# The two transfers that carry a batch's split row maxima are issued from GpSimd in place of SyncE

## The reference

```
mod = silu(c) @ wmod  ->  sa, ca, ga, sb, cb, gb      (per batch; |ga|, |gb| at least 0.25)
h = layernorm(x) * (1 + ca) + sa
q, k, v = h @ W_qkv.T, in 16 heads of 8 features
s = q k.T / sqrt(8) - slope[head] * (j - i), causal mask
x = x + ga * (softmax(s) v) @ W_o.T
h = layernorm(x) * (1 + cb) + sb
x = x + gb * moe(h)
moe: layer norm, router softmax over 8 experts, expert 0 with W1, W2, the other
     seven with one common perturbed pair W1', W2' (the largest and smallest 5% / 2
     of the entries by size changed by 0.8 of themselves); gelu between them
```

## Time and profile before

| what | value |
|---|---|
| median of 3 runs | 331.47 us (329.23 to 332.78) |
| profiled execution, its own time | 329.19 us |
| its span in the trace | 327.4 us |
| mean granted TensorE clock | 0.868 |
| busy: PE / DVE / ACT / POOL | 229.8 / 213.2 / 151.3 / 127.2 us |
| DMA, mean over the span | 62 GB/s |

### The profile page before, as it was taken

The page is one execution under the profiler, slowest core; times in us unless marked ns, Lnnn a source line. Parts: engine busy times, 40 slices in busy tenths (PEclk is TensorE's granted clock), DMA queues, the critical chain, the costliest instruction groups (busy, mean ns, idle before and its releaser), DMA issues.

```text
span 327.4 us, 5318 instructions
## 1 busy us (share of the span) xinstructions
PE 229.8 (70%) x1785; PEld 154.5 (47%) x1799; DVE 213.2 (65%) x681; ACT 151.3 (46%) x337; POOL 127.2 (39%) x204
## 2 busy tenths in 40 slices
PE   2741775288178456739739748878598399999995
PEld 1330554166056334617526625544335166767675
DVE  1662999469447818927955784699958548656264
ACT  1211433258256627716745664584454264343430
POOL 8320499227126314302511421234362582606050
PEclk9999995569879959966985985899879589999999
DMA  7737572502502500430250250000000000101011
GB/s 209 165 82 204 146 243 81 147 0 67 146 0 58 149 7 1 132 82 2 74 136 2 64 149 1 2 3 2 2 2 1 2 0 1 34 1 35 0 32 32
DMA packets 17551, 20.43 MB, mean 62 GB/s; under 512 B 1445, under 2 KB 15412, under 8 KB 16316
## 3 DMA queue, kind: packets, MB, share of 16 engines
q1 hardware_dynamic: 15476, 19.11, 21.8%
q10 hardware_dynamic: 2048, 0.98, 1.1%
HBM read 14.70 MB, written 5.26 MB: 61 GB/s over the span
## 4 chain that ended last, share of the span: by engine, by line
PE 40%; DMA 24%; DVE 15%; POOL 9%; SPq 6%; issue 4%; ACT 2%; POOLq 0%; DVEq 0%
DMA Qs<-nmT 13%; PE bank L746 9%; PE bank L728 9%; DMA parts<-part 6%; PE bank L653 4%; DVE msk L939 4%; SPq L275 3%; DVE nmax L970 3%; POOL hid L390 3%; PE bank L632 2%; DMA Ks<-parts 2%; DMA w_sb<-in_w 2%; PE bank L808 2%; PE bank L627 2%; PE bank L610 2%
## 5 line engine op out<-in xcount | busy, mean ns | idle before, releaser
L403 POOL TENSOR_SCALAR_AFFINE_SELECT PT<-PT 128x256 f32<-128x256 f32 (+1 forms) x96 | 47.3, 496 | 118.2 <-ACT PT L453 116.0
L970 DVE TENSOR_REDUCE nmax<-bank 128x2 f32<-128x512 f32 x64 | 43.8, 684 | 48.4 <-PE bank L610 48.3
L453 ACT ACTIVATE PT<-bank 128x512 f32<-128x512 f32 x96 | 53.9, 587 | 39.1 <-PE bank L627 36.8
L627 PE MATMUL bank<-Qs,Ks 80*128 80x128 bf16 x128 | 14.5, 244 | 38.1 <-DMA Qs<-nmT 38.1
L374 POOL TENSOR_TENSOR ex<-eul,lg 128x32 f32<-128x32 f32 x4 | 21.7, 5427 | 27.9 <-DVE lg L1030 27.9
L610 PE MATMUL bank<-Ks,Qs 78*128 78x256 bf16 x128 | 30.0, 323 | 0.0
L627 PEld LDWEIGHTS bank<-Qs,Ks 80*128 80x128 bf16 x128 | 10.0, 109 | 40.8 <-DMA Qs<-nmT 39.2
L632 PE MATMUL bank<-Qs,Ks 80*128 80x256 bf16 x128 | 28.5, 309 | 0.7 <-ACT PT L453 0.5
L606 PE MATMUL bank<-mask 128*128 128x256 bf16 x64 | 20.5, 320 | 10.4 <-DVE nmax L970 9.8
L653 PE MATMUL bank<-PT,Vx 128*32 128x256 f32 x256 | 24.0, 452 | 5.4 <-POOL PT L403 5.2
L966 DVE TENSOR_REDUCE nmax<-bank 128x4 f32<-128x512 f32 x32 | 21.7, 678 | 8.6 <-PE bank L603 8.6
(11 more groups left out here) (179 smaller groups left out, 503.6 us busy)
## 6 DMA issues: line engine op xcount, KB each, us to landing
Qs<-parts SPq DMA_DIRECT2D x8, 576.0 KB
Ks<-parts SPq DMA_DIRECT2D x8, 576.0 KB
parts<-part SPq DMA_DIRECT2D x8, 384.0 KB, 2.8
rows_bc<-rows_out SPq DMA_DIRECT2D x4, 512.0 KB, 7.2
parts<-part SPq DMA_DIRECT2D x8, 128.0 KB, 3.1
out<-ob SPq DMA_DIRECT2D x3, 256.0 KB, 2.3
x_all<-in_x ACTq DMA_DIRECT2D x5, 128.0 KB, 7.6
w_sb<-in_w SPq DMA_DIRECT2D x2, 256.0 KB, 6.8
```

The source lines that it names most:

```text
L403: gp.affine_select(out=v, in_=v, compare_op=ALU.is_ge, fill=0.0, base=0, pattern=[[0, v.shape[1]], [1, P]], channel_multiplier=-1).then_in ...
L453: act.activation(PT[:, e % 2, j], psE[u % 2][:, :], ACT.Exp).then_inc(q["exp_done"], 1)
L627: last = mm(bank[:, i * P:(i + 1) * P], Ks[0:R_E, r, h, P:S], Qs[0:R_E, r, h, P:S], start=True, stop=True, skip_group_check=True)
L970: ve.tensor_reduce(nmax[:, b % 2, 1, h:h + 2], bank.rearrange("p (h k) -> p h k", h=2), axis=AX.X, op=ALU.max, negate=True).then_inc(q["ma ...
```

## The change

`mrows` goes from SP's stream into GpSimd's. The wait and both transfers are the same ones, on the same bytes and the same semaphores. In GpSimd's loop the call stands after `lower_parts` and before `rstd` and `gate`, so at t = 4b+4 it comes behind the three masks of that step.

```
@@ SP
-            def mrows(b):
-
-                sp.wait_ge(q["nmlo_done"], b + 1)
-                sp.dma_start(Qs[R_S:R_S + 1, ROT(b)], nmT[:, b % 2, 0, :]).then_inc(mrow_in[b % 2], 16)
-                sp.dma_start(Qs[R_S + 1:R_E, ROT(b)], nmT[:, b % 2, 1, :]).then_inc(mrow_in[b % 2], 16)
-
             for t in range(T_FIRST, T_END):
-                b = batch_at(t, AT_NMT)
-                if b is not None:
-                    mrows(b)
                 b = batch_at(t, AT_SPLIT)
                 if b is not None:
                     stack(b)
@@ GpSimd
+            def mrows(b):
+
+                gp.wait_ge(q["nmlo_done"], b + 1)
+                gp.dma_start(Qs[R_S:R_S + 1, ROT(b)], nmT[:, b % 2, 0, :]).then_inc(mrow_in[b % 2], 16)
+                gp.dma_start(Qs[R_S + 1:R_E, ROT(b)], nmT[:, b % 2, 1, :]).then_inc(mrow_in[b % 2], 16)
...
                 if b is not None and b >= OWN_SPLIT:
                     lower_parts(b)
+                b = batch_at(t, AT_NMT)
+                if b is not None:
+                    mrows(b)
                 if t in LN1_AT:
```

## The result

| | before | after |
|---|---|---|
| median | 332.12 us (4 runs, 329.23 to 334.92) | 302.61 us (4 runs, 301.41 to 304.92) |
| profiled execution: its own time, its span | 329.19, 327.4 us | 301.41, 299.6 us |
| mean granted clock | 0.868 | 0.901 |

The ratio is 0.9146, 95% interval 0.9054 to 0.9238: 29.5 us less between the medians, 27.8 between the two spans. The forecast was 299.5 us, 32 less, in a range of 288 to 320.

The account below looks back on a forecast made before the run. The prediction took TensorE's 38.1 us of waits for the row maxima transfers as the bound. Waits gone 29.1, plus clock 3.5, less GpSimd's cost 1, made about 32 us: 331.5 to 299.5 us, range 288 to 320.

Parts of the forecast that it names:

- What bounds the kernel: Row maxima transfers, 13% of the span, make TensorE wait six times at a batch's first E unit, 38.1 us together.
- Two delays in series: Batch 1's maxima are issued 4.0 us late by SP's order, then lie 6.87 us behind the stack in SP's queue.
- rival 2: DMA engines, not the queue, hold the maxima while a stack is ahead or beside: 12.7 us saved, 319 us, chance 0.10.
- P: Moment GpSimd can issue, low part there and masks through: TensorE arrives 3.66 us later, in batch 0 1.5 us.
- T: Time from P until both maxima transfers land: two issues of 1.0 plus 2.8 landing, 4.8 us, ends 2.6 and 8.2.
- The clock: TensorE keeps its fast clock after short waits: 1.4 us in each of five batches, 7 us, half counted, 3.5.
- What GpSimd pays: Two issues at P add 2 us and delay the next masks some 0.7 us, mostly covered: 1 us of loss booked.
- The third: VectorE's two counts of 0.75 us around P hold up GpSimd's issues: 9 us lost, 308.5 us, chance 0.08.
- The fourth: The stack lands 2 us or more later and S units wait for it: 13 us less gain, 312 us, chance 0.05.
- The fifth: Issuing on GpSimd is long, 5.43 us each at P: kernel 19.5 us slower, 351 us, chance 0.07.

Follow-up runs that it names:

- sp_first: Kernel before, with SP sending the maxima on its own queue between the stack's parts going out and the stack's return: 289.75 us, ratio 0.879.
- pool_behind: Changed kernel, with GpSimd waiting for the stack's parts and doing small writes, so both stack returns are issued before the maxima: 333.71 us.
- pool_ahead: Changed kernel, with SyncE returning stack(b+2) only after the maxima of batch b have landed: 291.96 us, ratio 0.8791.
- sp_middle: Kernel before, on SyncE alone, with the maxima sent between the returns of Qs and Ks, so half the stack is ahead: 308.97 us.

## Why the prediction was right, and where it was not

**What bounds the kernel.** Right: the waits for the maxima are the largest removable share. With all six gone (sp_first) the kernel gains 40 us, near the 38.1 us of waits.

**Two delays in series, and the change goes round both.** This is the step that was half wrong. The change goes round SP's order. It does not go round the bytes: the prediction took "SP's queue" for what holds the 8 KB up, and the kernel with GpSimd behind the stack shows that it is what was issued before, on either queue. The rows of the kernel before could not part the two, since stack and maxima were on one queue there. The gain came only from being earlier than the stack or level with it, which the prediction had as a by-product. The prediction's own sign for rival 2, landings above 6 us, came in two of the six batches, 0 and 5.

**P.** Right. Taking GpSimd's first issue as P, TensorE arrived 3.73 us after it in batch 2 (104.22 against 100.49) and 3.70 in batch 5 (164.73 against 161.03); forecast 3.66. Batch 0: 1.64 (60.41 against 58.77); forecast 1.5.

**T.** The mean was near, the make-up wrong. An issue on GpSimd costs 0.48 to 0.76 us, near SP's 0.50 to 0.60, not 1.0. The second transfer's landing is not 2.8 but one of three: 1.9 to 2.2 ahead, 4.6 to 4.7 level, 7.2 to 7.3 behind. From P to the landing that makes 7.9 and 7.8 us in batches 0 and 5 (66.7 less 58.77; 168.85 less 161.03), 5.3 and 5.1 in 2 and 4, and about 2.7 in 1 and 3: a mean of 5.2 against 4.8. A single price for six batches came near the sum because it lies near the mean of three cases, and that is luck: had both streams met as in batches 0 and 5 every time, `pool_behind` shows that nothing would have been gained. The waits left were 13.6 us, forecast 9.0, so 24.5 us of them went and not 29.1.

**The clock.** Forecast 3.5 us. After a wait of 1.46 us TensorE stays at its 2.4 GHz level, after 6.37 and 4.17 it runs at 1.2, as the stretches of the changed kernel show (the granted clock is the third figure from the end; compare):

```profile
66.78:71.00 4.22, 4.22 (x20) 3.41 (x21) 2.43 (x9) 1.68 (x3) 1.84 (x4) 0.50 0.00 0
...
145.75:150.00 4.25, 4.09 (x43) 2.93 (x43) 3.65 (x12) 2.58 (x7) 1.45 (x3) 1.00 0.40 104
168.90:172.20 3.30, 3.30 (x27) 1.79 (x28) 0.04 (x1) 1.36 (x3) 0.64 (x1) 0.50 0.00 0
```

From the first E unit of batch 4 to the second S unit after it took 11.12 us before (171.08 to 182.20) and 8.59 after (145.75 to 154.34). Its start and end before, and its end after:

```profile
171.08 0.61 PE L627 MATMUL bank<-Qs,Ks 80*128 80x128 bf16 x4 [5.43 <-DMA Qs<-nmT]
...
182.20 0.39 PE L603 MATMUL bank<-Ks,Qs 78*128 78x128 bf16 x4
...
154.34 0.39 PE L603 MATMUL bank<-Ks,Qs 78*128 78x128 bf16 x4
```

In batch 5, whose wait stayed at 4.17, it took 11.56 and 11.54. Over the six batches this is 4.2 us less. With the 24.5 of waits that makes 28.7. TensorE came to its first E unit 1.2 us later than before, ahead of its wait there (60.41 against 59.23); 28.7 less 1.2 is 27.5 of the 27.8 us between the spans.

**What GpSimd pays.** 1.0 to 1.3 us an issue pair, hidden; no wait for its masks grew (5.2 us before and after). The 1 us booked was too much.

**The rivals.** The second, shared DMA engines, was given 0.10, and its mechanism is true: it holds fully in batches 0 and 5. Its price was wrong, because "within 1.3 us of the stack's issue" hid who goes first: a landing takes 4.7 us level and about 2 ahead. The rule of the Trainium skill, DMA: Bandwidth & Descriptors, "Issuing engines are not separate DMA queues", that transfers of all issuing engines run on the same 16 DMA engines, fits the square of queue and order. The same page says in "Queues, rings and completion order" that each DMA engine takes turns between the queues it has work for, a packet at a time. The trace does not bear this out as a way past the stack: 24 of the 32 packets of the maxima went only as the stack ended (`pool_behind`, 90.34 to 90.97 against 90.94). Why they got no turn before is open. The third, VectorE holding up the issues, fell: the two issues of batch 1, from 80.93 on, took 0.61 and 0.49 us with VectorE's two counts running from 80.30 to 81.71. The fourth showed only in another kernel, pool_ahead, once, at 1.6 us. The fifth fell by the price of an issue.

## What to carry to other kernels

Where a small transfer that something waits for stands behind large ones, issuing it before them is worth trying first, and another queue is not a substitute: look in the trace for what was issued in the few us before it on every queue, and move the issue, not the issuer. Where two streams issue without an order between them, the small transfer's time depends on which comes first; forecast it case by case (ahead, level, behind) and not by one mean price. Here splitting SP's own stage in two gave 40 us, and handing the transfers to another engine 29.5.

## What the runs showed of the hardware that was not expected

- 8 KB in 16 pieces on a queue of its own landed 6.5 us after its issue (median, at most 7.5) when 1152 KB had been issued up to 2.7 us before on another queue (batch 0 of pool_behind: 57.65 and 60.34). On SyncE's queue it took 4.7 us behind 576 KB (sp_middle), and on either queue 1.7 to 2.0 us at the median with nothing ahead (sp_first, pool_ahead).
- The bytes themselves were held up, not the report of their landing: in batch 1 of pool_behind 24 of the 32 packets started at 90.34 to 90.97, as the stack's last packet ended (90.94), and 8 at 86.33 to 86.88, in the midst of it.
- Issuing such a transfer from GpSimd took 0.48 to 0.76 us, from SyncE 0.50 to 0.60 in the kernel before; in sp_first two of SyncE's sixteen took 1.60 and 1.22.
